# SiLU of one tile's gate moved from ScalarE to GpSimd in an attention and FP4 feed-forward layer

## The reference, cut to what matters

```
x_proj = silu(x @ W1 + b1);  u, v, q, k = split(x_proj, 4)
scores = einsum(qh, kh)                     # 16 heads of 8, 2048 x 2048 each
av     = einsum(silu(scores) / 2048, vh)    # no softmax: a SiLU of every score
y      = layernorm(av * u, gamma, beta) @ W2 + b2
x      = layernorm(x + y)

gate = fp4_linear(x, w_gate); up = fp4_linear(x, w_up)   # 128 -> 352
h    = silu(gate) * up
x    = layernorm(x + fp4_linear(h, w_down))              # 352 -> 128
```

## Time and profile before

| what | value |
|---|---|
| median of three runs | 515.42 us |
| the profiled execution | 514.83 us, span 513.0 us |
| PE busy | 495.9 us (97%) |
| ACT busy | 487.4 us (95%) |
| DVE busy | 281.4 us (55%) |
| POOL busy | 56.9 us (11%) |

### The profile page before, as it was taken

The page is one execution under the profiler, slowest core; times in us unless marked ns, Lnnn a source line. Parts: engine busy times, 40 slices in busy tenths (PEclk is TensorE's granted clock), DMA queues, the critical chain, the costliest instruction groups (busy, mean ns, idle before and its releaser), DMA issues.

```text
span 513.0 us, 20141 instructions
## 1 busy us (share of the span) xinstructions
PE 495.9 (97%) x9030; PEld 263.9 (51%) x9032; DVE 281.4 (55%) x738; ACT 487.4 (95%) x548; POOL 56.9 (11%) x148
## 2 busy tenths in 40 slices
PE   9899999999999999999999999999999999999996
PEld 5443344444353444434354444434477777777762
DVE  6546642755748475665847475574343443544445
ACT  5999999999999999999999999999999999999940
POOL 7620000001010100101010100101010101101010
PEclk9999999999999999999999999999999999999999
DMA  7932340000000000000000000000000000000000
GB/s 190 231 85 60 96 134 3 1 3 7 3 6 3 8 2 3 6 1 8 3 7 3 8 1 3 6 4 6 3 8 4 9 4 10 9 3 9 4 3 12
DMA packets 15156, 12.39 MB, mean 24 GB/s; under 512 B 1783, under 2 KB 14718, under 8 KB 15070
## 3 DMA queue, kind: packets, MB, share of 16 engines
q1 hardware_dynamic: 14088, 9.44, 7.5%
q0 software_dynamic: 688, 1.40, 1.1%
q10 hardware_dynamic: 294, 0.26, 0.2%
HBM read 1.92 MB, written 1.05 MB: 6 GB/s over the span
## 4 chain that ended last, share of the span: by engine, by line
ACT 51%; PE 31%; issue 15%; DVE 2%; POOL 0%; POOLq 0%; DVEq 0%
ACT attn L643 50%; PE ps L405 29%; PE ps L419 2%; PE ps L448 1%; ACT v_sb L643 0%; POOL rstd_b L388 0%; DVE xn_b L769 0%; DVE stats_b L799 0%; ACT feat L643 0%; DVE xn_b L777 0%; DVE xn_b L773 0%; DVE xn_b L775 0%; POOLq L141 0%; DVE magic_b L771 0%; POOL ve_b L387 0%
## 5 line engine op out<-in xcount | busy, mean ns | idle before, releaser
L643 ACT ACTIVATE attn<-ps 128x1024 f32<-128x1024 f32 x512 | 475.8, 1211 | 0.3 <-PE ps L405 0.2
L405 PE MATMUL ps<-attn,v_pad 128*32 128x256 f32 (+1 forms) x5120 | 274.4, 341 | 0.3 <-DVE wdown_t L979 0.2
L405 PE MATMUL ps<-q_stack,k_stack 64*128 64x256 bf16 (+1 forms) x2560 | 173.6, 251 | 10.4 <-ACT attn L643 1.5
L405 PEld LDWEIGHTS ps<-attn,v_pad 128*32 128x32 f32 x5120 | 132.2, 109 | 80.2 <-issue 39.6
L405 PEld LDWEIGHTS ps<-q_stack,k_stack 64*128 64x128 bf16 x2560 | 78.6, 94 | 133.5 <-ACT attn L643 87.1
L387 POOL TENSOR_TENSOR ve_a<-mv_a,eps_col 128x1 f32<-128x1 f32 x24 | 4.6, 191 | 230.2 <-DVE mv_a L801 230.2
L387 POOL TENSOR_TENSOR ve_b<-mv_b,eps_col 128x1 f32<-128x1 f32 x24 | 4.6, 191 | 202.7 <-DVE mv_b L801 202.7
L742 DVE CAST parts<-feat 128x512 bf16<-128x512 f32 (+1 forms) x10 | 3.8, 383 | 25.3 <-ACT feat L643 25.3
L405 PE MATMUL ps<-zeros 128*128 128x512 bf16 x46 | 12.2, 412 | 1.4 <-DVE zeros L916 1.2
L388 POOL TENSOR_TENSOR rstd_a<-ve_a,minus_half 128x1 f32<-128x1 f32 x24 | 13.3, 555 | 1.9
L388 POOL TENSOR_TENSOR rstd_b<-ve_b,minus_half 128x1 f32<-128x1 f32 x24 | 13.3, 555 | 1.9
(11 more groups left out here) (183 smaller groups left out, 405.6 us busy)
## 6 DMA issues: line engine op xcount, KB each, us to landing
q_stack<-parts SPq DMA_DIRECT2D x18, 128.0 KB, 2.4
k_stack<-parts SPq DMA_DIRECT2D x15, 128.0 KB, 3.8
x_sb<-in_L_attn_x SPq DMA_DIRECT2D x3, 256.0 KB, 5.1
k_stack<-zeros SPq DMA_DIRECT2D x6, 128.0 KB, 5.4
q_stack<-zeros SPq DMA_DIRECT2D x6, 128.0 KB, 2.4
k_stack<-parts SPq DMA_DIRECT2D x9, 64.0 KB, 2.7
q_stack<-parts SPq DMA_DIRECT2D x9, 64.0 KB, 2.0
out<-x_a SPq DMA_DIRECT2D x8, 64.0 KB, 1.5
```

The lines of the kernel that those rows point to most:

```text
L405: return pe.matmul(to, lhsT, rhs, start=start, stop=stop, skip_group_check=True)
L643: return act.activation(to, frm, ACT.Silu, **kw)
```

## The change

ACT does not do the SiLU of the gate of tile 9 any more. DVE copies the gate from PSUM to `gate_b` (`copy_gate`). POOL makes the sigmoid from it with four instructions on 128 x 352 values: the larger of gate and -80; 1/e to that power; plus 1; that to the power -1. DVE multiplies `up` by the gate into a spare buffer, waits for the sigmoid (`sigmoid_ready`), multiplies with it, and quantises as before. The sigmoid stands in POOL's program before the third `rstd` of tile 9. The `hqT` job moves from step +30 to +31, and `down` from +31 to +33. Two memsets of 128 x 1 make the constants at the start.

```diff
+    BY_POOL = WIDE - 1
...
+    TILE_AT[BY_POOL] = (BEGIN[BY_POOL // 2 + 1], ODD | {"hqT": 31, "down": 33})
...
     ACT_JOBS = [k for k, (kind, i, tile) in enumerate(JOBS)
-                if kind in ("k", "q", "v", "u") or (kind == "gate" and tile is not None and tile not in BY_VEC)]
+                if kind in ("k", "q", "v", "u") or (kind == "gate" and tile is not None and tile not in BY_VEC and tile != BY_POOL)]
...
+            pool.memset(one_over_e[:, :], 0.36787944117144233)
+            pool.memset(minus_one[:, :], -1.0)
...
+            def sigmoid(r):
+
+                pool.wait_ge(job_by_vec, VEC_JOBS.index(job_no[("gate", 0, BY_POOL)]) + 1)
+                link(pool.tensor_scalar(r.xn[:, :], r.gate[:, :], -80.0, None, ALU.max))
+                link(pool.tensor_tensor(r.magic[:, :], one_over_e[:, 0:1].broadcast_to([P, FF]), r.xn[:, :], ALU.pow))
+                link(pool.tensor_scalar(r.magic[:, :], r.magic[:, :], 1.0, None, ALU.add))
+                pool.tensor_tensor(r.xn[:, :], r.magic[:, :], minus_one[:, 0:1].broadcast_to([P, FF]),
+                                   ALU.pow).then_inc(sigmoid_ready, 1)
+
             for tile in range(TAIL - 1):
                 for which in range(3):
+                    if tile == BY_POOL and which == 2:
+                        sigmoid(ROWS[tile % 2])
                     rstd(ROWS[tile % 2], which)
...
+            def copy_gate(tile):
+                bank = wait_made("gate", 0, tile)
+                dve.tensor_copy(ROWS[tile % 2].gate[:, :], ps[:, bank, 0:FF]).then_inc(job_by_vec, 1)
+                wait_taken("gate", 0, tile)
+
+            def gated_by_pool(tile):
+
+                r = ROWS[tile % 2]
+                spare = r.hqT[:, :, :].rearrange("p t n -> p (t n)")[:, 0:FF]
+                bank = wait_made("up", 0, tile)
+                dve.tensor_tensor(spare, r.gate[:, :], ps[:, bank, 0:FF], ALU.mult).then_inc(job_by_vec, 1)
+                wait_taken("up", 0, tile)
+                dve.wait_ge(sigmoid_ready, 1)
+                link(dve.tensor_tensor(r.gate[:, :], spare, r.xn[:, :], ALU.mult))
+                quantised_h(r)
```

More of the change, by code:

```diff
@@ L153, in build @@
         minus_half = sb("minus_half", [P, 1])
+        one_over_e = sb("one_over_e", [P, 1])
+        minus_one = sb("minus_one", [P, 1])
         eps_col = sb("eps_col", [P, 1])
@@ L232, in build @@
         xq_ready, hq_ready = sem("xq_ready"), sem("hq_ready")
+        sigmoid_ready = sem("sigmoid_ready")
         before_tail_down, tail_z, tail_y = sem("before_tail_down"), sem("tail_z"), sem("tail_y")
@@ L994, in _ @@
                     activate_gate(tile)
+                elif kind == "gate" and tile == BY_POOL:
+                    copy_gate(tile)
+                elif kind == "up" and tile == BY_POOL:
+                    gated_by_pool(tile)
                 elif kind == "up" and tile in BY_VEC:
```

## The result

The changed kernel takes 626.36 us (median of four runs, 625.16 to 626.39) against 516.21 us before (a fourth execution, 517.0 us, came to the three of the table above): 1.2131 times as long, 95% interval 1.2103 to 1.2159. The forecast was 515.8 us, no change that could be measured, with a range up to 562: the measured time is 64 us above the end of the range. The two powers on GpSimd take 56.5 us each, and nearly all of that is a stop of the whole kernel. All times and ratios are of undisturbed executions; one comparison, the last, had two disturbed ones (534.97 us for the kernel before, 1127.22 us for the other), which are left out.

What follows compares the result with a forecast made beforehand. ACT's work on the scores was taken to bound the kernel: 0.37 us gained, 0.7 lost at tile 10's job, 0 at `hqT`, +0.33 us on the profiled execution, giving 515.8 us on the median; range 514.4 to 562.

Steps and rivals of the forecast that it cites:

- What bounds the kernel: ACT is saturated by the scores from first to last; PE follows with a little lead; others matter only where ACT lacks scores.
- Part 1: On ACT, the gate's ACTIVATE of tile 9 goes, and ACT gains 0.37 us, the whole gain of the change.
- Part 2: POOL makes tile 9's sigmoid before `hqT` needs it: 7.1 us left for two powers taking 5.5, so no stall.
- P: Time of one power on POOL over 128 x 352, taken as 2.8 us; bounds 1.2 to 128 us.
- rival B: Powers cost tens of ns an element and PE stops at `hqT`: 527.9 us, span 518 to 570; chance 0.35.
- C: On POOL nothing of the power overlaps from element to element: +249.5 us, 765 us; chance 0.15.
- The page's estimate: From the skill's GPSIMD page: at best 30 ns an element, a power of 11.2 us and a stall of 15.3 us.
- The deadline: Sigmoid ready at 368.9 so `hqT` may begin at 373.3; POOL has 8.3 us, 7.1 of it for the two powers.
- Part 3: Moved `down` delays `zu` on DVE; PE waits at tile 10's first job and ACT stands 0.7 us (0 to 1.6).
- Costed at nothing: PE's matmuls, DVE's copy and second product, tile 9's third `rstd` behind the sigmoid, and POOL's two memsets add no time.

Runs made afterwards that it cites:

- `zu` first: Kernel before with tile 9's SiLU by VectorE's polynomial, `hqT` at +31, `down` at +33, `zu` made ahead of that `down`: 517.12 us, ratio 1.0006.
- the kernel with narrow powers: Changed kernel with both powers on 8 of the 352 columns, the rest of the sigmoid left out: 516.21 us, ratio 1.0019.
- third kernel: Kernel before with tile 9's SiLU by VectorE's polynomial, `zu` made ahead of `down`, `hqT` at +32, `down` at +33: 516.87 us, ratio 1.0015.

## Why the prediction was wrong, and where it was right

**What bounds the kernel**: right, but for one place: at step +32 PE had no lead left, and ACT had waited for it. Every difference found is a time that ACT stood, or an overlap that it lost, and PE, DVE and POOL count only where they cause that.

**Part 1, 0.37 us gained by ACT**: confirmed. The moves alone cost 1.40 us and the moves without ACT's instruction 1.06; the difference is 0.34. The pace used for it, 0.917 us, is an average over a stretch with the late ACTIVATE of +32 in it; the other distances are 0.90.

**Part 2, the sigmoid**: this is the step that failed, in one term, "Between these ends far apart I take the nearest row of a hard function on a full tile: DVE's reciprocal". It gave P = 2.8 us; P is 56.47. The row of another engine said nothing of this one. The power's own row had the answer inside its bounds: of the 364 ns above the add, about 200 are paid once and 160 for each column. The upper bound (P = 128 us) took all 364 for each column and was too high by 2.3; the price at which the total leaves 0.5% was 11 ns a column, and only a price that was almost wholly paid once could have stayed below it. That ought to have settled the ranking: rival B's mechanism and place were exactly right (PE's wait at `hqT` behind DVE's wait for the sigmoid), but its span ended at P = 30 us and C stood for over 100, and the measured 56.5 fell into the gap between two rivals, although the text called this one price unknown by a factor of 200. The range took its upper end, 562, from B and ended 64 us short.

The page's estimate of 11.2 us, from the Trainium skill's "GPSIMD Engine Reference", sections "Elementwise — side-by-side cycle accounting" and "Performance pitfalls for Q7 kernels", pointed the right way and was five times too low: at that page's clock of 1.2 GHz 160 ns are 192 cycles a column, far above the 36 that three operations a cycle would give for the 109 operations that the estimate supposed; no run shows how many there are.

The deadline was 2.1 us too generous. The max and the plus 1 take 1.20 and 1.18 us with their signals, not 0.6 each (1.2 us); and I took the ACTIVATE at 373.73 for the last of step +31, while it is the first of step +32. ACT does the gate of +24 behind the first half of +25, and the ACTIVATE at 373.73 is the 14th after it, so that start belongs to the half at which I put 374.65. With both, the powers had 7.1 - 1.2 - 0.9 = 5.0 us, and 112.9 - 5.0 = 107.9 us of stop, against 108.5 measured. What was not priced is PE's clock behind a long stop: 0.5 us between the transposes and ACT's start, which closes that gap, and 1.0 us in the two stops after it.

**Part 3, tile 10's first job**: right in mechanism and place, +1.40 us instead of 0.7. The same miscount of one ACTIVATE, 0.9 us, makes up for more than the difference, and the instants on DVE and PE, within 0.4 us, take some of it back. The 0.34 us that the moved jobs give back at +32 was in no term. The term's high end, 1.6, covered it. `zu` first removes it, which shows the cause.

**Costed at nothing**: DVE's copy and products and the memsets left no mark (the kernel with narrow powers has them all, and its +1.06 us is that of the moves less ACT's gain); the third `rstd` behind the sigmoid is harmless only while the sigmoid is short, as the kernel that does not await it shows.

Not tried: the powers spread over several stretches of POOL's idle time. By the price of 0.16 us a column POOL's idle time between two tiles, some 25 us, holds one power of about 150 columns, and both powers together need 113 us. So they could be hidden only if tile 9's `hqT` stood some 100 us later; this is worked out from the price, and no run shows it.

## What to carry to other kernels

An operation that the trace shows on one column only has a price for each column between zero and its whole excess over a cheap one; here 160 of the 364 ns were paid for each column. If the kernel stands or falls with that price, a row of another engine does not stand in for it; one run with two widths in an idle time of the engine settles it. Rivals must meet each other: a range between two of them that belongs to neither is a hole in the forecast. And a job that is moved towards a chunk's end moves all that stands behind it in its engine's queue; here the 0.37 us gained on the busiest engine was spent nearly four times over by a `zu` that came 2 us late.

## What the runs showed of the hardware

- A power on GpSimd costs 160 ns for each column and about 0.35 us once, whether it has 1, 16, 64 or 128 partitions (10.55, 10.55, 10.55, 10.57 us for 64 columns).
- On 128 x 352 a max or an add of a constant took GpSimd 1.11 and 1.10 us, an add of two tiles 0.94 us; DVE's TENSOR_SCALAR of the same size takes 0.34 us. On GpSimd one input was not cheaper than two.
- In the stop of 108 us without a matmul the granted clock went to 0.50, 1.2 GHz, and PE worked at it for some 3.8 us before it was back at 1.00; behind stops of 52 and 54 us it was 5.2 and 5.5 us.
- ACT's lost time is not all in its idle time: in the kernel before ACTIVATEs of 128 x 1024 have records of 1.02 to 1.61 us, 1.21 in the middle, but begin 0.90 us apart where nothing is late, and late scores made that 1.24 us (before, at 373.73) and 1.29 us (third kernel, at 379.20) with no idle time shown.
